# Attention loops over 16 batches written out with constants, in a four-layer fused block on one Trainium2 core

## What is computed

```python
x = L0(x, cond, ctx)   # attention of one head over ctx, then 3 experts and a gate
x = L1(x, ctx, cond)   # x += cross attention, 16 heads of 8, over the normalised and modulated ctx
x = L2(x, cond, ctx)   # self attention, cross attention over the normalised ctx, MLP
x = L3(x, ctx, cond)   # self attention, cross attention over ctx itself, MLP
# an attention, per batch and head:
attn = softmax(q @ k.T / sqrt(8));  out = attn @ v
```

## Time and profile before

| | us |
|---|---|
| median of 3 runs | 1877.32 |
| lowest, highest | 1859.43, 1903.56 |
| the profiled execution | 1865.84 |
| its span, first to last instruction | 1864.0 |
| TensorE busy | 1602.6 (86%) |
| VectorE, ScalarE, GpSimd busy | 1134.4, 1001.6, 656.4 |

### The profile page before, as it was taken

How to read it: one execution, slowest core, us unless ns; L and a number is a source line. 1 busy time by engine, 2 the same in 40 slices (tenths; PEclk the granted TensorE clock), 3 DMA queues, 4 the chain that set the end, 5 groups by cost and what they waited for, 6 DMA issues and landing times.

```text
span 1864.0 us, 54314 instructions
## 1 busy us (share of the span) xinstructions
PE 1602.6 (86%) x20495; PEld 1017.8 (55%) x20495; DVE 1134.4 (61%) x2291; ACT 1001.6 (54%) x1912; POOL 656.4 (35%) x898
## 2 busy tenths in 40 slices
PE   7888878698999997785999999987785899999986
PEld 4655534265666665433566666664342466666653
DVE  4554353676777773553777777752453777777742
ACT  2343232275777774231577777752241477777761
POOL 4000416065666623346366666400233122222200
PEclk9999888598999997896799999967786799999987
DMA  7222022344444431005445544320005444554310
GB/s 195 67 83 66 17 58 58 78 114 114 124 128 126 123 94 41 1 1 128 102 125 132 138 130 125 99 73 1 0 2 123 104 126 129 132 142 125 98 40 10
DMA packets 180138, 166.43 MB, mean 89 GB/s; under 512 B 69119, under 2 KB 169666, under 8 KB 180002
## 3 DMA queue, kind: packets, MB, share of 16 engines
q1 hardware_dynamic: 178418, 163.45, 34.2%
q10 hardware_dynamic: 1008, 1.05, 0.2%
q0 software_dynamic: 576, 0.02, 0.0%
HBM read 114.46 MB, written 40.08 MB: 83 GB/s over the span
## 4 chain that ended last, share of the span: by engine, by line
PE 64%; ACT 10%; DVE 9%; issue 6%; DMA 4%; SPq 4%; POOL 2%; ACTq 0%; DVEq 0%; POOLq 0%
PE PS L1169 11%; PE PS L1063 8%; PE PS L1195 8%; PE PS L1057 7%; PE PS L896 6%; PE PS L1143 5%; PE PS L1052 3%; SPq L432 3%; PE PS L980 3%; ACT q_parts L829 3%; PE PS L1269 2%; DVE mx L1575 2%; PE PS L1000 2%; ACT v_sb L763 2%; DMA k_dram<-k_lo 2%
## 5 line engine op out<-in xcount | busy, mean ns | idle before, releaser
L1575 DVE TENSOR_REDUCE mx<-PS 112x1 f32<-112x500 f32 x1152 | 715.8, 671 | 241.4 <-PE PS L1143 236.4
L829 ACT ACTIVATE q_parts<-PS 125x448 f32<-125x448 f32 x1152 | 562.1, 544 | 114.2 <-PE PS L1195 111.3
L577 POOL CAST k_hi<-k_full 128x500 f16<-128x500 f32 x144 | 87.4, 607 | 641.3 <-issue 330.2
L612 POOL TENSOR_SCALAR cx<-cx,norm_b 125x128 f32<-125x128 f32 x384 | 303.9, 805 | 26.5 <-issue 18.0
L1195 PEld LDWEIGHTS PS<-q_st,k_st 50*125 50x125 f16 x4608 | 185.8, 139 | 212.3 <-ACT q_parts L829 146.6
L1143 PE MATMUL PS<-k_st,q_mx 50*112 50x500 f16 x1152 | 262.3, 402 | 42.3 <-DMA q_mx<-q_all 38.1
L1195 PE MATMUL PS<-q_st,k_st 50*125 50x112 f16 x4608 | 262.4, 235 | 38.8 <-ACT q_parts L829 22.1
L1169 PE MATMUL PS<-q_parts,v_sb 125*18 125x112 f32 x9216 | 293.3, 271 | 0.0
L1169 PEld LDWEIGHTS PS<-q_parts,v_sb 125*18 125x18 f32 x9216 | 219.5, 101 | 52.0 <-issue 42.9
L579 POOL TENSOR_TENSOR k_lo<-k_full,k_hi 128x500 f16<-128x500 f32 x144 | 163.8, 1138 | 21.1 <-POOL k_hi L577 4.4
L763 ACT ACTIVATE v_sb<-PS 125x512 f32<-125x512 f32 x144 | 86.9, 603 | 104.8 <-PE PS L1063 104.7
(11 more groups left out here) (269 smaller groups left out, 2003.0 us busy)
## 6 DMA issues: line engine op xcount, KB each, us to landing
k_st<-k_dram SPq DMA_DIRECT2D x864, 62.5 KB, 2.2
cx<-in_ctx SPq DMA_DIRECT2D x56, 672.0 KB
k_dram<-k_hi SPq DMA_DIRECT2D x144, 125.0 KB, 1.8
k_dram<-k_lo SPq DMA_DIRECT2D x144, 125.0 KB, 1.9
v_sb<-in_ctx SPq DMA_DIRECT2D x8, 672.0 KB
q_mx<-q_all SPq DMA_DIRECT2D x48, 99.8 KB
q_st<-q_all SPq DMA_DIRECT2D x48, 99.8 KB
cx<-in_ctx SPq DMA_DIRECT2D x56, 78.0 KB
```

The source lines that it names most:

```text
L612: last = pool.tensor_scalar(cx[:, p, c, :], cx[:, p, c, :], norm_b[:, p, 0, c:c + 1], norm_b[:, p, 1, c:c + 1], ALU.subtract, ALU.mult)
L829: act.activation(probs[:, c % RING, u * HR:(u + 1) * HR], PS[0:KC, (2 * c + u) % SC_RING, 0:HR], ACT.Exp).then_inc(sem("exp_done"), 1)
L1575: dve.tensor_reduce(mx[:, r, t:t + 1], PS[0:PW, MX_BANK + u % MX_RING, 0:TK], AX.X, ALU.max)\
```

## The change

Both helpers lose their hardware loop; the body is called once for each batch with plain numbers. The sequence of matmuls, activations, copies, DMAs and semaphores is the same, batch by batch.

```diff
             first((0, 0, 0))
-            for b in range(PEELED):
-                both((b, b // 2, b % 2), (b + 1, (b + 1) // 2, (b + 1) % 2), SELF_AHEAD[b])
-            with eng.Fori(PEELED // 2, B // 2 - 1) as i:
-                both((2 * i, i, 0), (2 * i + 1, i, 1), [])
-                both((2 * i + 1, i, 1), (2 * i + 2, i + 1, 0), [])
-            both((B - 2, B // 2 - 1, 0), (B - 1, B // 2 - 1, 1), [])
+            for b in range(B - 1):
+                both((b, b // 2, b % 2), (b + 1, (b + 1) // 2, (b + 1) % 2), SELF_AHEAD[b] if b < PEELED else [])
             last((B - 1, B // 2 - 1, 1))
...
-            def at(b, i=None):
-                return (b, b // 2, b % 2) if i is None else (2 * i + b, i + b // 2, b % 2)
+            def at(b):
+                return (b, b // 2, b % 2) if b < B else None
 
             first()
-            for b in range(2):
+            for b in range(B):
                 body(*[at(b + k) for k in range(4)])
-            with eng.Fori(1, B // 2 - 2) as i:
-                for b in range(2):
-                    body(*[at(b + k, i) for k in range(4)])
-            for b in range(B - 4, B):
-                body(*[at(b + k) if b + k < B else None for k in range(4)])
```

## The result

Over 20 runs each, the changed kernel takes 1888.69 us in the median (1875.38 to 1901.71) and the kernel before 1864.28 (1851.86 to 1903.56). The ratio is 1.0126, with a 95% interval of 1.0095 to 1.0157. It is slower by somewhat more than 1%: inside the range that was given, but not the 1866 of the forecast. 1888.7 is close to where rival B stood (1886.3). The prediction took 2% as the least that a measurement would tell; with 20 runs of each it tells 0.3%. The 1877.32 shown ahead of the prediction was a median of only three runs.

A forecast was written before the change was run, and what follows sets the result against it. TensorE, busy 86% of the span, plus what stops it was taken to bound the kernel. From the profiled 1865.84 us, -9.65 - 10.55 - 1.1 + 21.8 gave 1866.3, forecast as 1866 us, range 1838 to 1896.

The forecast's parts named there:

- rival B: SyncE becomes the bound at `unit`'s wait for `k_stacked`, all layers like layer 1: 1886.3 us, 1903.5 with clock falls; chance 0.15.
- term 4: Cross attentions: instruction fetches slow SyncE's batch to 23.45 us, so TensorE waits for keys in batches 4 to 11; +21.8 us.
- Term 1: Cross attentions: TensorE's loop register instructions go, shortening five looped pairs of batches in each layer; -9.65 us.
- The doubt about the missing context loads: Term 1's written-out batches 12 and 13 lack context loads; if the relief came from that, the term would be 0.
- Term 2: Layer 1, batches 3 and 4: TensorE's slow loop branch, its 5.11 us gap and the lower clock behind go; -10.55 us.
- Term 3: Self attention: twelve looped batches in two layers gain half of 0.18 us each when written out; -1.1 us.
- A: Full gain: fetches seldom meet SyncE's DMAs, keys come early, terms 1 to 3 remain; 1844.5 us, chance 0.25.
- C: TensorE itself starves on fetching some 66 more blocks; at 0.5 us each +33, 1878 us beside A's gains; chance 0.05.
- D: Nothing on the path changes: registers were hidden, the slow branch one execution's accident; 1866 us, chance 0.55 together with the forecast.

The follow-up runs named there:

- the kernel with keys on time: The changed kernel with SyncE's key DMAs reordered (write 0, write 1, read 0, write 2, read 1): 1848.39 us, ratio to the kernel before 0.9881.
- the two padded kernels: The kernel before with 16 or 32 unused one-column matmuls (64 or 128 instructions) added early on TensorE: 1867.74 us (0.9984) and 1872.11 us (1.0001).

## Why the forecast failed

The forecast failed at term 4, the price of late keys: it was set at 21.8 us and measured at 31.6 to some 46, by how it is counted. The terms that were to bring time came out as they were given, together: the kernel with keys on time stands at 0.9881, 22 us below before, where terms 1 to 3 sum to -21.3.

*Term 1, registers (-9.65).* Right. 682.0 - 671.3 = 10.7 us, measured with keys on time on both sides. The doubt about the missing context loads beside batches 12 and 13 is answered too: batches 8 and 9 reach the same 45.25, 44.62 and 44.49 with the loads beside them.

*Term 2, the slow branch (-10.55).* Right for the traced execution. Terms 1 and 2 together were -20.2, and 671.3 - 694.3 = -23.0 was measured, some 2 us of it waits for keys that before has itself. But as a term for the kernel before it rested on one trace: the two padded kernels, in which no branch was slow, are no faster than before. How many of its runs have the gap is not shown, so that the sum of terms 1 to 3 agrees with the medians may be in part luck.

*Term 3, self attention (-1.1).* Too small to be told: 0.9876 (0.9797 to 0.9954) without it, 0.9881 with it, and the first interval is some 15 us to either side.

*Term 4, late keys (+21.8).* This is the step that failed, by its size. The mechanism and its signs were right: q8 at exactly 160 packets and 2.62 MB, SyncE's batch at 24.1 us in layer 1 and 23.2 in layers 2 and 3 where 23.45 was forecast, no wait for GpSimd in layer 2, and waits of L1134 for `k_st` of 21.1 us where "some 20" were. But batches 2 to 11 went up from the 671.3 us of timely keys to 702.9, **+31.6**; between the two spans (1836.9 and 1874.9) it is 38.0 us, and by the ratios 0.9881 and 1.0126 some 46. By layers, with what the sum holds for each (8 x 0.8 - 1, 8 x 1.1 - 1, 8 x 1.2 - 1) and what the traces show batch by batch:

| layer | forecast | measured | of it waits for `k_st` | of it lost behind a wait, at the low clock |
|---|---|---|---|---|
| 1 | 5.4 | 14.8 | 9.0 | 5.2 |
| 2 | 7.8 | 8.4 | 4.2 | 2.9 |
| 3 | 8.6 | 8.4 | 5.5 | 1.6 |

(The remaining 2.5 us of the 21.1 us of waits lie in batch 12, and 3.4 of the 31.6 us are not assigned.) Two things were left out. The first is what comes behind a wait, 9.6 us. The batches 4 and 10 of layer 1 and 4 of layer 2 have waits of 1.2, 2.6 and 2.0 us and granted clocks of 0.87 to 0.88, a stretch of the 1.2 GHz level. Against 23.2, 23.1 and 22.7 us in the kernel of timely keys they take 26.98, 28.28 and 27.60, together 13.9 more, 5.8 of it wait. Not every wait does this: 1.7 us in batch 6 of layer 1 and 2.0 in batch 12 of layer 3 left the clock at 1.00. The prediction had this fall, at 5.7 us a layer, but only in rival B. It gave it to waits caused by the dearest SyncE, when the 5.11 us gap of before had already shown that a gap brings it. The second is that one mean, 24.06, was used for three layers whose rows read 24.9, 23.8 and 23.4. The row of layer 1 less 0.6 is 24.3, close to the 24.1 that was measured there, and 8 x 1.6 - 1 would have been 11.8 in place of 5.4. In layers 2 and 3 the forecast is right by luck: waits of 4.2 and 5.5 where 7.8 and 8.6 were forecast, and the clock on top.

*The sum.* 694.3 - 23.0 + 31.6 = 702.9 accounts for +8.6 of the 10.9 us between the spans. The remaining 2.3 lie outside these batches, where both signs occur: the first batch of layer 1 takes 26.2 us against 23.6, batch 14 of layer 2 19.4 against 26.5 with its low clock.

*The rivals.* A fell with the late keys; in another order of SyncE's DMAs it is what happens. B is near the measured median, and has its mechanism, SyncE as the bound: late keys and falls of the clock behind them. But its premise that all layers behave like layer 1 did not hold, layers 2 and 3 stayed at 23.2, and its 1886.3 leaves the clock out: that the number fits so well is luck. C is excluded: with 160 blocks fetched, the batches of the reordered kernel are as short as any of before. D is excluded by term 1 and by the two ratios, 1.0126 and 0.9881.

*The rule cited.* "Runtime: NRT & Kernel Launch" of the Trainium skill, section "Instruction fetch mechanics", says that crossing a block is mostly hidden. For the engine that fetches this trace agrees (45.25, 44.62, 44.49 us a pair with fetches). As a forecast of the kernel's time it failed here, since the price is paid by SyncE: 1.0136 with 16.4 KB transfers and 1.0029 with 4 bytes. Its taken branch that forces a fetch stall is seen here at about 5 us and with nine more blocks fetched, at one, none or seven of the twelve branches that jump back.

*What stays open.* The median of after is 12 us above its profiled execution, and that of before 1.6 below. The granted clock explains little of it: 0.890 in the median of the 20 runs, 0.893 in the profiled one. Whether other runs have longer waits for keys was not traced. The medians bear the mechanism out nevertheless: only the order of DMAs separates after (1.0126) from 0.9881, and only TensorE's code of the cross attentions separates before from 1.015.

## What to carry to other kernels

When straight code replaces a loop, look at every queue that issues DMAs, and not only at the engine whose code grows: compare the longest issue, and the length of that queue's batch, in stretches with and without instruction fetches, and ask whether the queue still has a lead. A queue that waits for its own write before it issues the next thing is where such a cost lands; putting the next independent write ahead of the read gave 2.4% here (0.9881 against 1.0126) and made the written-out code pay. Price a wait in front of TensorE together with the stretch at the lower clock that can follow it: 13.9 us for 5.8 us of waits in three batches, while others of 1.7 and 2.0 us cost their own length. And do not take one mean over layers whose own rows differ by more than the margin that decides (24.9, 23.8 and 23.4 us against TensorE's 22.3 to 22.7).

## What the runs showed that was not expected

- A one-row transfer of 16.4 KB, or an instruction fetch of 16 KB, can make another engine's DMA issue take 1 to 2 us in place of 0.43: 64 of 864 in after, each with a fetch under way. Three such transfers a batch in the looped kernel cost 1.4%, three on top of the change's own fetches 3.7%.
- A TensorE loop of two batches, about six blocks of 16 KB (straight code has 29 or 30 fetches in ten batches), ran without fetches in its steady turns, except behind a slow branch; with four batches it fetched 167 blocks, more than straight code.
- The back branch of the same loop takes 0.215 us, or 5 with nine blocks fetched anew (97 = 88 + 9, 154 = 91 + 7 x 9). None, one or seven of the twelve that jump were slow in kernels whose loop does the same, and 64 unused instructions ahead of it changed 1.0205 to 0.999.
- Moving two key writes ahead of the reads before them left the long issues as they were (64 and 61 over 0.9 us) and yet removed every one of 23 waits.
